# The second half of W prepared in chunks inside the first pass, by way of DRAM

## The reference

```python
def reference(x, itok, w, W_base, b_base, W_gate, A, B):   # x: [32, 128, 2048]
    y = einsum('bct,bcd->bdt', x, w[itok])                 # a 128x128 matrix per batch entry
    result = einsum('bnd,od->bno', y, W_base) + b_base     # 2048 x 2048
    probs = softmax(einsum('bnd,ed->bne', y, W_gate))      # 8 experts, the best 2 kept, renormalised
    h = einsum('bnd,erd->bner', y, A) * route_w[..., None] # rank 16 each
    return x + result + einsum('bner,eor->bno', h, B)
```

## Time and profile before

| | |
|---|---|
| median of 3 runs | 1634.38 us |
| the profiled execution, outside | 1634.34 us |
| its span on the core | 1632.6 us |
| TensorE, VectorE, ScalarE, GpSimd busy | 94%, 80%, 37%, 39% |
| mean granted TensorE clock | 0.972 of full |
| DMA | 201.87 MB, 124 GB/s in the mean |

### The profile page before, as it was taken

One profiled execution on the slowest core, in us unless ns is written; L12 is line 12 of the kernel. 1 busy time (PEld: TensorE's weight loads), 2 busy tenths in 40 slices (PEclk: granted clock), 3 DMA queues, 4 the chain that ended last, 5 costly groups with the idle time before them and its releaser, 6 DMA issues.

```text
span 1632.6 us, 25730 instructions
## 1 busy us (share of the span) xinstructions
PE 1536.8 (94%) x9539; PEld 837.8 (51%) x9539; DVE 1300.2 (80%) x2228; ACT 596.5 (37%) x996; POOL 631.9 (39%) x473
## 2 busy tenths in 40 slices
PE   5667999999999999999668999999999999999998
PEld 5444555555555555555464555555555555555553
DVE  6666888888888888888776888888888888888874
ACT  6654333333333333333583323333322333332231
POOL 2534455555555555555453122222212221221222
PEclk8788999999999999999889999999999999999999
DMA  5332444444444444444731344343334434333432
GB/s 198 130 117 82 128 136 136 135 135 134 128 136 136 136 127 133 132 134 125 235 104 39 98 137 136 110 122 121 102 91 136 136 113 121 122 105 88 134 107 71
DMA packets 102911, 201.87 MB, mean 124 GB/s; under 512 B 10874, under 2 KB 24186, under 8 KB 102266
## 3 DMA queue, kind: packets, MB, share of 16 engines
q1 hardware_dynamic: 102786, 200.22, 39.8%
HBM read 128.96 MB, written 71.22 MB: 123 GB/s over the span
## 4 chain that ended last, share of the span: by engine, by line
PE 89%; DVE 5%; ACT 2%; issue 2%; DMA 1%; POOL 1%; POOLq 0%; SPq 0%; DVEq 0%; ACTq 0%
PE bank_x L1121 10%; PE bank_x L1122 10%; PE bank_x L1123 10%; PE bank_y L1123 10%; PE bank_y L1122 10%; PE bank_y L1121 10%; PE bank_z L1121 3%; PE bank_z L1123 3%; PE bank_z L1122 3%; PE bank_h L1122 3%; PE bank_h L1121 3%; PE bank_h L1123 3%; PE bank_c L1121 2%; PE bank_c L1123 2%; PE bank_c L1122 2%
## 5 line engine op out<-in xcount | busy, mean ns | idle before, releaser
L475 POOL TENSOR_TENSOR x_res<-x_res,t_sums 128x512 f32<-128x512 f32 x256 | 350.7, 1372 | 895.6 <-DVE t_sums L827 735.5
L1121 PE MATMUL bank_x<-TT,s_parts 128*128 128x512 f16 x768 | 295.5, 385 | 14.8 <-POOL TT L450 7.5
L1122 PE MATMUL bank_x<-TT,s_parts 128*128 128x512 f16 x768 | 295.0, 384 | 0.0
L1123 PE MATMUL bank_x<-TT,s_parts 128*128 128x512 f16 x768 | 294.6, 384 | 0.0
L1121 PE MATMUL bank_y<-TT,s_parts 128*128 128x512 f16 x768 | 291.2, 379 | 0.0
L1122 PE MATMUL bank_y<-TT,s_parts 128*128 128x512 f16 x768 | 291.1, 379 | 0.0
L1123 PE MATMUL bank_y<-TT,s_parts 128*128 128x512 f16 x768 | 291.1, 379 | 0.0
L571 ACT ACTIVATE p_copies<-bank_x,y_inv 128x512 f32<-128x512 f32 x128 | 87.8, 686 | 492.8 <-PE bank_x L1123 398.7
L827 DVE TENSOR_TENSOR t_sums<-t_sums,inv_w 128x512 f32<-128x512 f32 x256 | 218.6, 854 | 8.8
L800 DVE TENSOR_TENSOR s_parts<-a_full,s_parts 128x512 f16<-128x512 f32 x224 | 208.1, 951 | 7.5 <-ACT s_parts L556 7.5
L456 POOL TENSOR_TENSOR x_res<-x_res,BT 128x512 f32<-128x512 f32 x128 | 197.8, 1545 | 4.8 <-DMA x_res<-in_x_dram 3.3
(11 more groups left out here) (219 smaller groups left out, 2715.6 us busy)
## 6 DMA issues: line engine op xcount, KB each, us to landing
x<-in_x_dram SPq DMA_DIRECT2D x32, 1024.0 KB, 5.7
x_res<-in_x_dram SPq DMA_DIRECT2D x128, 256.0 KB, 3.7
part_scratch<-x_res SPq DMA_DIRECT2D x128, 256.0 KB, 2.9
x_res<-part_scratch SPq DMA_DIRECT2D x128, 256.0 KB, 3.9
out_dram<-x_res SPq DMA_DIRECT2D x128, 256.0 KB, 2.8
x_parts<-in_L_ffn_W_base_dram SPq DMA_DIRECT2D x12, 512.0 KB, 5.3
a_full<-in_L_ffn_W_base_dram SPq DMA_DIRECT2D x12, 512.0 KB, 4.8
w_cond<-in_L_cond_weights_dram SPq DMA_DIRECT2D x64, 64.0 KB, 3.9
```

Of the source, the lines that this page charges most:

```text
L475: nc.gpsimd.tensor_tensor(XR[:, xr_slot(m), :], XR[:, xr_slot(m), :], TM[:, m % 2, :], ALU.add).then_inc(r_added, 1)
L1121: nc.tensor.matmul(dst, lhs[0], rhs[0], start=start, stop=False, skip_group_check=chained)
L1122: nc.tensor.matmul(dst, lhs[0], rhs[1], start=False, stop=False, skip_group_check=chained)
L1123: return nc.tensor.matmul(dst, lhs[1], rhs[0], start=False, stop=stop, skip_group_check=chained)
```

## The change

Units 8 to 15 after step 15 are gone. In their place each of the steps 1 to 15 has a window of two chunks of 128 columns of a unit (step 7 has the whole fourth unit, four chunks). At the end of the step before, SP loads rows of W into `XP`; where a unit begins, ScalarE sums the rows' absolute values and VectorE makes the scales, and TensorE spreads the inverse ones; ScalarE scales the rows in place. In the step itself, each chunk is turned by four plain f32 transposes into `bank_d`, copied into half of `AF`, added up in four subtractions (a step's first chunk on VectorE, the others on GpSimd), rounded in one ScalarE instruction of 128x896, split in one of VectorE, and both parts go to DRAM (`wt_dram`), in runs of 128 f16, that is 256 bytes, for each partition and sum. The inverse scales go to `inv_dram`. In step 15 and at its end, ScalarE's queue issues 14 loads of 1 MB from `wt_dram` into TT, each when the last product with that part of TT is done, and products of step 16 wait for their own. FT, BT, h_dram's first part and `inv_w` are loaded in step 15 instead of behind it. `SLOTS` goes from 10 to 9; hw, hwT, the diagonal, the first h and the three buffers for finished pieces share one tile (`late_words`). In the first pass ScalarE's copy U2 of s = 1 stands ahead of S3's upper part.

In the order SP, GpSimd, ScalarE, VectorE, TensorE:

```diff
-SLOTS = 10
+SLOTS = 9
+WHOLE = 3
+    wt_dram = nc.dram_tensor("wt_scratch", [NPROD, 2, P, 2, C4, Q], F16, kind="Internal").ap()
...
+            def store_piece(g, c, part):
+                s, r = g // 4, g % 4
+                sp.wait_ge((bg_hi, bg_lo)[part], n_chunk(g, c))
+                at = piece(g, c, part)
+                sp.dma_start(wt_dram[:, s, :, part, c, r * P:(r + 1) * P].rearrange("q p n -> p q n"), pieces[:, at, :, :]
+                             ).then_inc(bg_out[at], 16)
...
+                if chunks:
+                    if chunks[0] == 0:
+                        store_inv(g)
+                    store_piece(g, chunks[0], 0)
+                    store_piece(g, chunks[0], 1)
+                    store_piece(g, chunks[1], 0)
+                    if len(chunks) > 2:
+                        store_piece(g, chunks[1], 1)
                 for j in range(4 if n == 0 else 0, 8):
                     m = 8 * n + j
                     store_tile(m)
+                    if len(chunks) == 2 and j == 0:
+                        store_piece(g, chunks[1], 1)
...
+                    if n < len(WINDOWS) and j == (4 if n == 0 else 3):
+                        sp.wait_ge(cond_done, 4 * (n + 2))
+                        load_rows_ahead(*window_ahead(n))
...
+                    for c in chunks[1:3]:
+                        add_up(g, c)
                     add_bias(8 * n + begin)
...
+            def load_weights(s, q):
+                act.wait_ge(prod_done, n_prod(NP - 1, s, q))
...
+                act.dma_start(TT[:, q, s, :, :, :], wt_dram[SAVED.index(q), s, :, :, :, :]).then_inc(t_in[s][q], 16)
...
+                if chunks and chunks[0] == 0:
+                    copy_inv_ahead(g)
                 copy_p(n, 0, P1_COPY)
+                if chunks:
+                    copy_chunk(g, chunks[0])
+                    copy_chunk(g, chunks[1])
+                    upper_chunk(g, chunks[0])
                 copy_p(n, 0, P5_COPY)
+                if chunks:
+                    upper_chunk(g, chunks[1])
...
+            def scales_ahead(g):
+                dve.wait_ge(bg_sums, g + 1)
+                power_of_two(row_pow2[:, :], row_sum[:, 0, :], row_clamped[:, :])
...
+            def add_up_first(g, c):
+                chunk = full[c % 2].rearrange("p (i n) -> p i n", i=8)
+                dve.wait_ge(bg_copied, n_chunk(g, c))
+                nc.vector.tensor_tensor(chunk[:, 5, :], chunk[:, 2, :], chunk[:, 0, :], ALU.subtract)
+                link(nc.vector.tensor_tensor(chunk[:, 4, :], chunk[:, 0, :], chunk[:, 1, :], ALU.subtract))
+                link(nc.vector.tensor_tensor(chunk[:, 6, :], chunk[:, 2, :], chunk[:, 4, :], ALU.subtract))
+                nc.vector.tensor_tensor(chunk[:, 7, :], chunk[:, 6, :], chunk[:, 3, :], ALU.subtract
+                                        ).then_inc(bg_sum_first, 1)
...
+                if chunks:
+                    add_up_first(g, chunks[0])
                 features(n)
                 if more:
                     find_top(n + 1)
...
+                if chunks:
+                    lower_chunk(g, chunks[0])
                 finish(n, 0, C11)
                 if more:
                     scale_x(n + 1)
+                if chunks and not whole:
+                    lower_chunk(g, chunks[1])
...
+                if ahead_chunks and ahead_chunks[0] == 0:
+                    scales_ahead(ahead)
                 if n + 2 < NSTEP:
                     find_maxima(n + 2)
...
+                if n == NP:
+                    pe.wait_ge(t_in[s][q], 16)
...
+            def turn_chunk(g, c):
+                pe.wait_ge(bg_rows_scaled, n_window(g, c))
...
+                for i, (block_of, half) in enumerate(((1, 0), (0, 0), (1, 1), (0, 1))):
+                    mm = nc.tensor.transpose(BD[:, i * P:(i + 1) * P],
+                                             xp_rows[:, block_of, half * Q + c * P:half * Q + (c + 1) * P], ident[:, :])
+                mm.then_inc(bg_tr, 1)
...
                 product(n, 0, 0)
+                if chunks:
+                    turn_chunk(g, chunks[0])
                 make_features(n)
                 if more:
                     transpose_maxima(n + 1)
+                if chunks:
+                    turn_chunk(g, chunks[1])
...
-                if n == NP - 1:
-                    pe.wait_ge(p_copied, n_copy(n, 1, P4_COPY))
...
-                        w_quads(g)
+                if ahead_chunks and ahead_chunks[0] == 0:
+                    spread_ahead(ahead)
```

More of the change, by code:

```diff
@@ L294, in n_s, with n_chunk, piece, piece_turn @@
             return NPROD * n + q + 1
+        def n_chunk(g, c):
+            return C4 * g + c + 1
+        def piece(g, c, part):
+            return (2 * (C4 * g + c) + part) % NPIECE
+        def piece_turn(g, c, part):
+            return 16 * ((2 * (C4 * g + c) + part) // NPIECE + 1)
         def xr_slot(m):
@@ L512, in _ @@
                         add_r(8 * n + j)
+                        if j == 0 and len(chunks) > 2:
+                            add_up(g, chunks[3])
                 else:
@@ L515, in _ @@
                         add_r(8 * n + j)
-                if n == NP - 1:
-                    for g in range(NU, 2 * NU):
-                        w_lower(g)
         @block.scalar
@@ new lines, in scale_rows_ahead, with copy_inv_ahead @@
+            def scale_rows_ahead(g, chunks):
+                act.wait_ge(bg_scaled, g + 1)
+                for i in range(2):
+                    act.wait_ge(bg_rows[i], 16 * n_window(g, chunks[0]))
+                    rows = halves(xp_rows[:, i, :], chunks)
+                    ins = nc.scalar.activation(rows, rows, ACT.Copy, scale=row_scale[:, i:i + 1])
+                ins.then_inc(bg_rows_scaled, 1)
+            def copy_inv_ahead(g):
+                act.wait_ge(bg_spread, g + 1)
+                if g > 0:
+                    act.wait_ge(bg_inv_out, 16 * g)
+                nc.scalar.copy(inv_piece, BD[:, 0:2 * P]).then_inc(bg_inv, 1)
@@ new lines, in copy_chunk, with upper_chunk @@
+            def copy_chunk(g, c):
+                act.wait_ge(bg_tr, n_chunk(g, c))
+                if g == WHOLE and c >= 2:
+                    act.wait_ge(bg_lo, n_chunk(g, c - 2))
+                else:
+                    act.wait_ge(s_lo, NPROD * (n_window(g, c) + 1))
+                nc.scalar.activation(full[c % 2][:, 0:Q], BD[:, :], ACT.Copy).then_inc(bg_copied, 1)
+            def upper_chunk(g, c):
+                first_chunks = [(unit, chunks[0]) for unit, chunks in WINDOWS]
+                if (g, c) in first_chunks:
+                    act.wait_ge(bg_sum_first, n_window(g, c))
+                else:
+                    act.wait_ge(bg_sum, n_chunk(g, c) - n_window(g, c))
+                at = piece(g, c, 0)
+                if piece_turn(g, c, 0) > 16:
+                    act.wait_ge(bg_out[at], piece_turn(g, c, 0) - 16)
+                nc.scalar.activation(pieces[:, at, :, :], full[c % 2][:, P:8 * P].rearrange("p (q n) -> p q n", q=NPROD),
+                                     ACT.Copy).then_inc(bg_hi, 1)
@@ new lines, in load_weights @@
+            def load_weights(s, q):
+                act.wait_ge(prod_done, n_prod(NP - 1, s, q))
+                if s == 1 and q == 0:
+                    for part in range(2):
+                        act.wait_ge(bg_out[piece(NU - 1, C4 - 1, part)], piece_turn(NU - 1, C4 - 1, part))
+                    act.wait_ge(bg_out[piece(NU - 1, C4 - 2, 1)], piece_turn(NU - 1, C4 - 2, 1))
+                act.dma_start(TT[:, q, s, :, :, :], wt_dram[SAVED.index(q), s, :, :, :, :]).then_inc(t_in[s][q], 16)
@@ L710, in _ @@
                     nc.scalar.activation(hwT[:, 0, :], BD[:, 0:2 * P], ACT.Copy).then_inc(hwT_hi, 1)
+                if whole:
+                    copy_chunk(g, chunks[3])
                 if more:
@@ L713, in _ @@
                     split_x_hi(n + 1, 1)
+                if whole:
+                    upper_chunk(g, chunks[2])
                 copy_p(n, 0, P4_COPY)
+                if whole:
+                    upper_chunk(g, chunks[3])
+                if fresh:
+                    for q in range(4):
+                        load_weights(0, q)
                 if more:
@@ L1049, in _ @@
                 more, second = n + 1 < NSTEP, n >= NP
+                g, chunks = window_of(n)
+                whole = len(chunks) > 2
+                ahead, ahead_chunks = window_ahead(n)
+                if chunks:
+                    add_up_first(g, chunks[0])
                 features(n)
@@ L1063, in _ @@
                     split_x_lo(n + 1, 1)
+                if whole:
+                    lower_chunk(g, chunks[2])
                 finish(n, 0, C12)
+                if whole:
+                    lower_chunk(g, chunks[3])
                 if second:
```

223 lines of the change are left out of this document (168 added, 55 removed).

## The result

The changed kernel takes 1612.26 us (median of 4 runs, 1609.71 to 1614.3), the kernel before beside it 1634.33; the ratio is 0.9865, 95% interval 0.9848 to 0.9882. It is faster, but 26 us slower than the forecast of 1586, and 0.26 us beyond the range's end of 1612.

The account below looks back on a forecast made before the run. TensorE bounds the kernel, with a 75.6 us hole: 1634.3 - 75.6 = 1558.7; with 16 of TensorE work taken as 1575; + 7 + 1.5 + 2 + 1 = 1586.5, taken as 1586 us; range 1573 to 1612.

Parts of the forecast that it names:

- the forecast's own upper bound: Whole kernel: 1613 us, with 28 us for opening steps and 5 each for step 7 and the first window.
- The hole: Between steps 15 and 16: TensorE idles 73.6 us while W's second half is prepared, plus 2.0 slow; 75.6 us removed.
- TensorE's added work: Steps 1 to 15: 128 transposes at 0.11 us, 14.1, plus 1.6 for spreads; 16 us, all on the path.
- Opening steps: Steps that open a unit: first tile and x's split come late; 1.0 us for each of 7, 7 us (0 to 28).
- Step 7: The step with a whole unit: TensorE waits once, the fourth transposition for the third chunk's copy; 1.5 us (0 to 5).
- The first window: After step 0: TensorE waits for the first rows' diagonals; 1.7 us, taken as 2 (0 to 5).
- Stores: First pass, four a step in 256-byte pieces: 5 to 8 us of DMA time a step, hidden.
- First rival: First pass: DMA becomes the bound, stores and loads sharing one queue; 1605 us given, chance 0.10.
- The hand-over: Steps 15 and 16: 14 weight loads of 1 MB might arrive late; 1 us taken (0 to 36).
- the second rival: Steps 15 and 16: weights arrive late, price up to 36 us, 1621 us; chance 0.08.
- third rival: First pass: VectorE becomes the bound, six added instructions each waiting 1.73 us for GpSimd; 5.5 a step, 1658 us, chance 0.07.
- twice the mean packet: First pass stores below 512 B: if each piece cost this, the step would be 65 us, the kernel near 1920.

Follow-up runs that it names:

- experiment 1: Changed kernel without the 14 weight loads and the waits for them, so the second pass reuses W's first half: 1593.68 us, ratio 0.9758 to the kernel before.
- experiment 10: Against the kernel of experiment 9, VectorE does features and top search ahead of the first sums in steps that open a unit: 1592.18 us.
- experiments 2 and 8: Against the changed kernel: 2 puts step 7's second split later and one store earlier, 1608.77 us; 8 leaves out piece stores and weight loads, 1589.08 us.
- experiment 3: Changed kernel with each weight load issued as two, in runs of 2 KB instead of 8 KB, same queue and order: 1611.94 us.
- experiment 9: Changed kernel with weight loads on SP's queue, FT's load first, two second-half loads ahead of BT's, and step 7's split and store reordered: 1589.15 us.
- experiment 4: Changed kernel with FT's load issued at the head of step 15 in SP's queue: 1609.23 us, ratio 0.9849 to the kernel before.

## Why the prediction was off, point by point

The profiled execution is 26.9 us above the sum of 1586.5. By the periods the misses are: hand-over 17.1, step 7 6.0, start 2.0, opening steps 1.7, step 1 0.5, transposes and spreads -0.5. That makes 26.8. That the time lies so near the range's end is chance: the forecast's own upper bound (1613, and so above the 1612 given) was made of 28 us for the opening steps and 5 each for step 7 and the first window, with nothing added for the hand-over, where the loss came.

- **The hole, 75.6 us: right.** It is gone; without the loads step 16 follows step 15 in 42.53 us (experiment 1).
- **TensorE's added work, 16 us: right.** Four transposes stand in the place of 0.44 us (167.38 to 167.82); 32 such groups are 14.1. A steady step is 0.99 longer, 43.09 where 43.0 was said.
- **Opening steps, 1.0 us each: nearly right in size (1.14 to 1.17, once 1.82), half right in place.** I had the first tile and x's split late; the split is, for 0.4 us, and more than half is the top of the maxima, behind the first sums and their lock. In experiment 10 the top's wait is gone and the split's has grown to 1.26 us. VectorE's wait before the first tile shrank from 3.88 to 0.29 in step 15 and is gone in the opening step of 344.67 us, as said.
- **Step 7, 1.5 us (0 to 5): 7.5,** the 9.53 above a steady step less 0.88 for its transposes and 1.14 for the opening. I counted one wait, the fourth transposition for the third chunk's copy, and it is there, 1.15 us. I did not count the three buffers: a store's landing (3.2 us, and behind other issues of SP) is part of the chain from the fourth piece on. It is a wait that the change added, and it wasn't in my list. By experiments 2 and 8 it is 3.4 to 5.1 of the 7.5 us; 2.4 remain with all stores gone.
- **The first window, 2 us (0 to 5): 4.0.** The wait itself was 2.6; behind it come 1.35 us more, by the lower clock here and by a wait for VectorE's top in experiment 1. Neither was in the term. The term counted the scales alone, and not VectorE's work behind them.
- **Stores, 5 to 8 us hidden: hidden in all steps but step 7, and smaller,** 2.6 us a step, near the bound worked out from bytes (3 us) and far from that by packets (22.6). First rival: wrong.
- **The hand-over, 1 us (0 to 36): 18.1, and this is the step that failed.** I asked for the weights' own deadlines alone, and to those the answer was right: they were in time, and so the second rival is wrong too; that 18 us fall inside its 36 is luck, since they have another cause. Of the 18.1 us, 15.4 are the wait for FT and 2.6 the clock behind it. I had even written that the usual traffic goes on at 132 GB/s beside them. It did not: SP's queue got 4.38 MB in 50 us, 88 GB/s, with FT added to its work, and what it issued from 803 to 825 us landed 18 to 27 us later. TensorE stood for FT. I had also drawn the engines' rate too low (310 GB/s; 379 were moved at a share of 0.95), and with the right one the total would have looked safer still. The question that was lacking: who else waits in the other queue, and for how long is he served slowly?
  The Trainium skill, "DMA: Bandwidth & Descriptors", Queues, rings and completion order, states that each DMA engine goes round the queues that have work and takes a whole packet from each before it moves on. Taken with the trace (packets of 7.3 KB in one queue, of 1.4 KB in the other, from the two lines of the view), such turns would give the queue of long runs the larger part of the bytes, if a packet of the view is what the page calls one, which no run here shows. Experiment 3's shift from 23% to 34% points the same way, but isn't a proof of it, since there ScalarE's issues slowed as well. Shown is that the loads slowed SP's queue; by what rule is open.
- **VectorE and the lock, third rival: wrong as a bound, right as a mechanism.** In steps 2 to 15, two of the four first sums take 1.35 us, where the same two take 0.27 in the opening steps of experiment 10, and VectorE is busy in 39.81 of 43.09. The price was 1.1 us for each of these two, not 1.73 for each of six.

## What to carry to other kernels

A bulk transfer that is put on a second queue has two prices: whether it arrives in time, and what the queue beside it no longer gets while it runs; the second is read as the landing times of the other queue's rows, and the cure was here one queue in the order of the deadlines (experiment 9), not more and shorter runs (experiment 3) or one load moved up (experiment 4). When a step's work is doubled once (here a whole unit in step 7), count its buffers and the landing of what frees them, not only its instructions. And where TensorE is made to wait, look at the clock behind the wait: it took 2.6 us more at the hand-over, and nothing that counted in step 1, where another engine's chain was as long.

## What was not expected of the hardware

- With both hardware queues full, the one with the long runs took 77% of the bytes (14.56 of 18.95 MB), and the other's landings rose from 3 to 6 us to 18 to 24, at no higher total rate (379 GB/s) than one queue alone reaches (372).
- ScalarE's DMA issues are not free when many are under way: with 28 instead of 14, four of them took 9.99 us, and TensorE waited up to 8.89 us for the copies behind.
- The same subtraction of 128x128 in f32 took 0.27 or 1.35 us on VectorE, by whether a 128x512 addition of GpSimd ran beside it. The third and fourth, each waiting for the one before, took 0.43 to 0.47 in all steps.
- Stores in runs of 256 bytes (packets under 512 bytes rose from 10874 to 71898) landed in 3.2 us per 224 KB and took 2.6 us of the mean engine's time for four. The Trainium skill, "DMA: Bandwidth & Descriptors", Specifications, has transfers below 512 B off line rate and names no price. The price that the prediction tried for it, twice the mean packet, would have made the step 65 us; it is 43.09.
